# Attention and quantised FFN on one core: transposing x on TensorE, and weight quotients on GpSimd

## The reference

```
q = ctx @ Wq.T + bq ;  k = ctx @ Wk.T + bk          (512 x 128)
p = softmax(q @ k.T)                                (512 x 512)
x = x + layernorm(x) @ p.T
v = bf16(layernorm(x)) ;  h = bf16(layernorm_w_b(v))
h = bf16(quant(h) @ quant(W1).T + b1)               (512 x 2048)
h = gelu(h)
h = bf16(quant(h) @ quant(W2).T + b2)
x = x + bf16(v + h)
```

## Time and profile before

| | us |
|---|---|
| median of three runs | 285.61 (285.0 to 285.69) |
| the profiled execution | 283.25 |
| its span in the trace | 281.4 |
| busy: DVE | 249.2 (89% of the span) |
| busy: PE | 228.7 (81%) |
| busy: ACT | 169.4 (60%) |
| busy: POOL | 69.0 (25%) |

### The profile page before, as it was taken

The page is one execution under the profiler, slowest core; times in us unless marked ns, Lnnn a source line. Parts: engine busy times, 40 slices in busy tenths (PEclk is TensorE's granted clock), DMA queues, the critical chain, the costliest instruction groups (busy, mean ns, idle before and its releaser), DMA issues.

```text
span 281.4 us, 3244 instructions
## 1 busy us (share of the span) xinstructions
PE 228.7 (81%) x937; PEld 99.4 (35%) x946; DVE 249.2 (89%) x377; ACT 169.4 (60%) x287; POOL 69.0 (25%) x96
## 2 busy tenths in 40 slices
...
DMA packets 103077, 42.92 MB, mean 152 GB/s; under 512 B 93844, under 2 KB 96152, under 8 KB 102552
## 3 DMA queue, kind: packets, MB, share of 16 engines
...
## 4 chain that ended last, share of the span: by engine, by line
DVE 45%; PE 25%; ACT 11%; DMA 8%; issue 5%; POOL 4%; SPq 2%; ACTq 0%; DVEq 0%; POOLq 0%
DVE amax L764 12%; PE ps L722 9%; PE ps L712 8%; PE ps L661 4%; DVE w_int L807 4%; DMA xhl<-pf 3%; DVE hq L966 3%; DVE stats L918 3%; DMA wst<-in_L_ffn_W 3%; DVE vw L961 3%; DVE pf L871 3%; DVE phl L942 2%; DVE wquant L861 2%; POOL rs L350 2%; DVE xhl L954 2%
## 5 line engine op out<-in xcount | busy, mean ns | idle before, releaser
L661 PE MATMUL ps<-pT,xT 128*128 128x512 f16 x192 | 49.7, 414 | 14.1 <-DMA pT<-phl 11.0
L722 PE MATMUL ps<-w2T,xhl 128*128 128x512 bf16 x247 | 56.5, 379 | 2.9 <-DMA xhl<-pf 2.4
L712 PE MATMUL ps<-w1T,cxT 128*128 128x512 bf16 x256 | 58.0, 380 | 0.0
L558 ACT ACTIVATE wst<-ps 128x1024 bf16<-128x1024 f32 x32 | 32.3, 1019 | 27.9 <-PE ps L712 27.9
L764 DVE TENSOR_REDUCE amax<-phl 128x64 f32<-128x2048 bf16 x16 | 36.5, 2280 | 6.9 <-ACT phl L562 6.9
L649 PE MATMUL ps<-qkT 128*128 128x512 f32 x32 | 19.5, 715 | 22.7 <-ACT pf L457 18.8
L661 PEld LDWEIGHTS ps<-pT,xT 128*128 128x128 f16 x192 | 19.9, 106 | 48.0 <-issue 31.8
L722 PEld LDWEIGHTS ps<-w2T,xhl 128*128 128x128 bf16 x256 | 24.6, 98 | 33.2 <-DMA xhl<-pf 4.2
L712 PEld LDWEIGHTS ps<-w1T,cxT 128*128 128x128 bf16 x256 | 23.7, 98 | 32.6 <-issue 6.2
L562 ACT ACTIVATE phl<-wst 128x2048 bf16<-128x2048 bf16 x16 | 30.6, 1910 | 1.3
L423 POOL TENSOR_TENSOR wst<-wst,vs 128x512 bf16<-128x512 bf16 x12 | 14.8, 1233 | 55.5 <-DVE wquant L866 55.5
...
## 6 DMA issues: line engine op xcount, KB each, us to landing
wst<-in_L_ffn_W ACTq DMA_DIRECT2D x6, 1024.0 KB, 6.1
xs<-in_x SPq DMA_DIRECT2D x4, 1024.0 KB, 8.4
...
wst<-in_L_ffn_W SPq DMA_DIRECT2D x2, 1024.0 KB, 10.3
xhl<-pf SPq DMA_TRANSPOSE x17, 4.3
xT<-xhl SPq DMA_TRANSPOSE x16, 4.6
pT<-phl SPq DMA_TRANSPOSE x16, 3.3
```

Of the source, the lines that this page charges most:

```text
L558: act.activation(ys[:, k, 1024 * g:1024 * g + 1024], ps_y[:, 2 * g:2 * g + 2, :], ACT.Copy)\
L661: pe.matmul(ps_pv[:, t % 2, :], xT[:, t, NT * a + n, :], pT[:, :, NT * c + n, :], start=(s == 0), stop=False)
L712: last = pe.matmul(ps_y[:, c, :], h1T[:, k, t, :], w1T[:, 4 * c:4 * c + 4, t, :], start=False, stop=(t == KT - 1))
L722: last = pe.matmul(ps_z[:, k, :], h2T[:, k, t, :], w2T[:, t, :], start=False, stop=(t == FT - 1))
```

## The change

Three things are changed.

1. The transpose of normalised x. PE transposes the float32 tile `xn` in four blocks of 128 x 128 into PSUM (`transpose_x`), into `ps_xT`, which is banks 2 and 3, those of q and k. ACT then copies the high half from PSUM, and DVE subtracts from PSUM for the low half. The sixteen DMA transposes of x go. Batches alternate between two buffers, `xhl` and `xT`. `queries_keys(b)` now waits until all four `x_low` of the batch before have read the banks.
2. The weight quotients. POOL multiplies the quarter by the inverse scale in place and in float32 (`over_scale`, eight calls). DVE's clip reads that float32 and writes int16. `w_over` goes.
3. The orders. POOL's small factors stand in a new sequence with the quotients, and some of them behind a wait for a whole tail (`h_rdy`). ACT's `v` work is one step later in its loop. DVE takes the moments of the next batch in the middle of `front` and aggregates them near its end, and the tails follow the whole fronts. SP loads x of batches 2 and 3 behind the first transpose of p, not the last.

The core of the diff (PE, ACT, POOL, SP and the weight steps of DVE):

```diff
-W_STEPS = 7
+W_STEPS = 6
...
+xT_even = xhl[:, :, :, :].rearrange("p t a n -> p t (a n)").rearrange("p t (c l) -> p t c l", l=P)
+xTs = (xT_even, xT)
...
+ps_xT = ps[:, 2:4]
...
-        for t in range(LT):
-            wait_alone(sp, x_lo, b * LT + (t + 1), sp_gate)
-            wait_alone(sp, pv_ps, (b - 1) * LT + (t + 1), sp_gate)
-            sp.dma_start_transpose(xT[:, t, :, :], xhl[:, t, :, :].rearrange("p a n -> p (a n)"))\
-              .then_inc(xT_rdy[t], 16)
-            if ctx is not None and t == 0:
-                load_ctx(ctx)
+        if ctx is not None:
+            load_ctx(ctx)
         wait_alone(sp, pv_ps, b * LT, sp_gate)
         for t in range(NT):
             wait_alone(sp, p_lo, b * NT + (t + 1), sp_gate)
             sp.dma_start_transpose(pT[:, t, :, :], phl[:, t, :, :].rearrange("p a n -> p (a n)"))\
               .then_inc(pT_rdy[t], 16)
-        if later is not None:
-            load_x(later)
+            if later is not None and t == 0:
+                load_x(later)
...
+    def over_scale(a, u):
+
+        pool.wait_ge(w_step[a], W_STEPS * u + 4)
+        w = blocks(wst[:, a, :])
+        inverse = mxi[:, a, :, 0:1].broadcast_to([P, NB, BLOCK])
+        pool.tensor_tensor(w, w, inverse, ALU.mult).then_inc(w_u[a], 1)
+
+    over_scale(W1, 0)
...
+    pool.wait_ge(p_lo, NT)
+    over_scale(W2, 0)
+    over_scale(W1, 1)
+    factors_x(2)
+    mean_x1(0)
+    pool.wait_ge(p_lo, 2 * NT)
+    over_scale(W2, 1)
+    factors_x1(0)
+    over_scale(W1, 2)
+    factors_x(3)
+    factors_v(0)
+    mean_x1(1)
+    pool.wait_ge(h_rdy, LT)
+    over_scale(W2, 2)
+    factors_x1(1)
+    over_scale(W1, 3)
+    factors_v(1)
+    mean_x1(2)
+    pool.wait_ge(h_rdy, 2 * LT)
+    over_scale(W2, 3)
+    factors_x1(2)
+    factors_v(2)
+    mean_x1(3)
+    factors_x1(3)
+    factors_v(3)
...
+        act.wait_ge(xT_ps, b * LT + (t + 1))
+        wait(act, pv_ps, (b - 2) * LT + (t + 1))
+        act.activation(xTs[b % 2][:, t, 0:NT, :].rearrange("p n l -> p (n l)"), ps_xT[:, t % 2, :], ACT.Copy)\
+           .then_inc(x_hi, 1)
...
-        for t in range(LT + 1):
+        for t in range(LT + 2):
             if t < NT:
                 exp(front, t)
                 x_high(front, t)
-            if t > 0:
+            if 0 < t <= NT:
                 p_high(front, t - 1)
-            if b is not None and t > 1:
+            if b is not None and 1 < t < LT + 1:
                 x_plus(b, t - 2)
-            if t == 2 and b is not None:
+            if t == 1 and b is not None:
                 load_w2(front)
-            if v is not None and t > 0:
-                v_sums(v, t - 1)
-            if v is not None and t < LT:
-                v_out(v, t)
+            if t == LT and front + 1 < B:
+                load_w1(front + 1)
+            if v is not None and t > 1:
+                v_sums(v, t - 2)
+            if v is not None and 0 < t <= LT:
+                v_out(v, t - 1)
             if qk is not None and t == 2:
                 context(qk)
-        if not isinstance(front, int) or front + 1 < B:
-            load_w1(front + 1)
...
     def queries_keys(b):
+        wait(pe, x_lo, b * LT)
...
+    def transpose_x(b, t):
+        pe.wait_ge(xn_rdy, b * LT + (t + 1))
+        wait(pe, x_lo, b * LT + (t - 1))
+        for n in range(NT):
+            last = pe.transpose(ps_xT[:, t % 2, P * n:P * n + P], xn[:, t % 2, P * n:P * n + P], ident[:, :])
+        last.then_inc(xT_ps, 1)
...
-        pe.wait_ge(xT_rdy[t], 16 * (b + 1))
+        pe.wait_ge(x_lo, b * LT + (t + 1))
         wait(pe, x1_rdy, b * LT + (t - 1))
...
-        for t in range(LT):
-            if t < NT - 2:
-                energies(front, t + 2)
-            if b is not None:
-                values(b, t)
+        energies(front, 2)
+        transpose_x(front, 0)
+        transpose_x(front, 1)
+        if b is not None:
+            values(b, 0)
+        energies(front, 3)
+        transpose_x(front, 2)
+        if b is not None:
+            values(b, 1)
+        transpose_x(front, 3)
+        if b is not None:
+            values(b, 2)
+            values(b, 3)
...
-    def w_over(a, u):
-        dve.wait_ge(w_step[a], W_STEPS * u + 4)
-        inverse = mxi[:, a, :, 0:1].broadcast_to([P, NB, BLOCK])
-        dve.tensor_tensor(blocks(w_int[:, :]), blocks(wst[:, a, :]), inverse, ALU.mult)\
-           .then_inc(w_step[a], 1)
-
     def w_clip(a, u):
-        dve.wait_ge(w_step[a], W_STEPS * u + 5)
-        dve.tensor_scalar(w_int[:, :], w_int[:, :], QMAX, None, ALU.min).then_inc(w_step[a], 1)
+        wait(dve, w_step[1 - a], W_STEPS * (u + a))
+        dve.wait_ge(w_u[a], u + 1)
+        dve.tensor_scalar(w_int[:, :], wst[:, a, :], QMAX, None, ALU.min).then_inc(w_step[a], 1)
 
     def w_mult(a, u):
         wait(dve, (w1T_rdy, w2T_rdy)[a], 16 * u)
-        dve.wait_ge(w_step[a], W_STEPS * u + 6)
+        dve.wait_ge(w_step[a], W_STEPS * u + 5)
...
+    def x_moments(b):
+        dve.wait_ge(ld_x[b], 16)
         for t in range(LT):
             dve.bn_stats(stats[:, t, :], xs[:, LT * b + t, :]).then_inc(st, 1)
-        if isinstance(b, int) and b > 0:
+
+    def x_aggregate(b):
+        if b > 0:
             dve.wait_ge(rx_rdy, b)
+            dve.wait_ge(xn_rdy, LT * b)
         for t in range(LT):
             wait_alone(dve, st, LT * b + (t + 1), dve_gate)
             dve.bn_aggr(mv[:, t, :], stats[:, t, :]).then_inc(mvr, 1)
...
-        wait_alone(dve, x_lo, b * LT + (t - 1), dve_gate)
+        wait(dve, xT_ps, b * LT + (t - 1))
...
     def x_low(b, t):
         dve.wait_ge(x_hi, b * LT + (t + 1))
-        dve.tensor_tensor(xhl[:, t, 1, :], xn[:, t % 2, :], xhl[:, t, 0, :], ALU.subtract)\
-           .then_inc(x_lo, 1)
+        xt = xTs[b % 2][:, t, :, :]
+        dve.tensor_tensor(xt[:, NT:2 * NT, :].rearrange("p n l -> p (n l)"), ps_xT[:, t % 2, :],
+                          xt[:, 0:NT, :].rearrange("p n l -> p (n l)"), ALU.subtract).then_inc(x_lo, 1)
```

More of the change, by code:

```diff
@@ L168, in xattn_ffn_kernel @@
         nm, off_rdy = sem("nm"), sem("off_rdy")
+        w_u = [sem("w1_u"), sem("w2_u")]
         v_mean, v_mean2, v_ms = sem("v_mean"), sem("v_mean2"), sem("v_ms")
         rx_rdy = sem("rx_rdy")
-        xT_rdy = [sem(f"xT_rdy{t}") for t in range(LT)]
+        xT_ps = sem("xT_ps")
         pT_rdy = [sem(f"pT_rdy{t}") for t in range(NT)]
@@ L266, in _ @@
             front(1, 3, 3)
-            with sp.Fori(2, B) as b:
+            for b in range(2, B):
                 front(b)
@@ L399, in _ @@
             factors_x(1)
-            def batch(b, x, v):
-                if x is not None:
-                    factors_x(x)
-                if v is not None:
-                    factors_v(v)
-                mean_x1(b)
-                factors_x1(b)
-            batch(0, 2, None)
-            for b in range(1, B - 2):
-                batch(b, b + 2, b - 1)
-            batch(B - 2, None, B - 3)
-            factors_v(B - 2)
-            mean_x1(B - 1)
-            factors_x1(B - 1)
-            factors_v(B - 1)
+            pool.wait_ge(p_lo, NT)
[23 more added lines that the diff above has]
+            factors_v(3)
             def add_residual(i):
@@ L1015, in front @@
                 x_low(b, 2)
[L1016 to L1020 removed]
+                w_mult(W1, b)
                 recip(b, 3)
+                w_amax(W2, b)
+                recip_scaled(b, 3)
                 p_low(b, 2)
[L1024 removed]
+                w_power(W2, b)
                 x_low(b, 3)
[L1026 to L1049 removed]
+                w_scale(W2, b)
[4 more added lines that the diff above has]
+            def tail(b):
+                for t in range(LT):
+                    times_w(b, t)
+                    plus_b(b, t)
             def tail_parts(b):
```

86 lines of the change are left out of this document (12 added, 74 removed).

## The result

The changed kernel takes 300.91 us (median of four runs, 297.03 to 305.98) against 285.31 on the same chip: ratio 1.0537, 95% interval 1.0465 to 1.0608. The profiled execution took 300.17, its span is 298.4 against 281.4. Two of the changed kernel's four runs were in a slower state and are left out of the ratio. Executions of one kernel differ by several microseconds: those four lie within 9 us, and those of the kernel before lie within 1.5 us on this chip and within 6 on the chips of the experiments. A few tenths of a per cent between two kernels mean nothing, and the experiments are read by stretch, each from one profiled execution. T0 to T3 are the first `negmax` of the four batches, "last tile" is `x_plus(3,3)`.

The account below looks back on a forecast made before the run. Stage one was taken as a DVE queue with PE close behind, stage two as following PE. Terms 8.5 + 2.9 + 1.5 + 7.1 = 20.0 us on 283.25 gave 303.3, with 2.4 to the median 305.6; range 292 to 312.

Parts of the forecast that it names:

- Front 0: First batch's front: late first factors, late fourth exponential and q and k waiting for x_low move T1 by 8.5 us.
- The link: Between batches: q and k share PSUM banks with transposed x, so wait for the fourth x_low; 8.1 us to first energy.
- T1 to T2: Front 1: PE's in-order transposes, values, q and k, with a POOL hold on DVE, move T2 by another 2.9 us.
- T2 to T3: Front 2 and tail: ACT's later v_sums delay factors_v and the tail, moving T3 by 1.5 us.
- T3 to the last tile: Front 3 onward: POOL's last quotient and factors_x1(2) queue behind h_rdy, delaying ACT; +7.1 us.
- The sign "`x_plus(3,0)` over 20 us late": Entry of the last stretch on ACT: a delay over 20 us was to show the forecast right.
- Costed at nothing: PE's 64 blocks (8 us, up to 15), x loads (at most 8.4 us) and SP's sixteen shed transposes add nothing separately.
- DVE's saving is idle: DVE in stage one: the 3.5 us saved on it become idle time; net saving of work 14.0 us.
- The milder one: Rival: same chains without POOL holds on DVE (-5.4) and with PE at high clock at T1 (-2.7); 297.5 us, chance 0.25.
- The slow clip: Rival: DVE's clip reads float32 one element a step, 6.6 us more over three fronts; 312 us, chance 0.10.
- "Same": Rival: every new wait at its least, and the last stretch gives it back; 285 us, chance 0.04.
- "faster": Rival: DVE's queue still sets everything, 14.0 us less work minus 1.8 of first factors; 273.4 us, chance 0.05.

Follow-up runs that it names:

- e7_qk_banks: Changed kernel with q and k in PSUM banks 0 and 1 and no wait of queries_keys for the fourth x_low; ratio 1.052 to the kernel before.
- The relatives with the same front: Two variants of the changed kernel whose front 1 is unchanged, e1_factors_first and e6_v_step_early; T1 to T2 29.1 and 28.5 us.
- e9_before_pool_quotient: Kernel before with only the eight weight quotients moved to POOL in float32, x by DMA and orders of PE, ACT, SP untouched; ratio 1.028.
- e6_v_step_early: Changed kernel with ACT's v_sums and v_out one step earlier in its loop, as in the kernel before; ratio 1.049.
- e1_factors_first: Changed kernel with factors_x1(2) on POOL moved ahead of the wait for the tail and the last quotient; ratio 1.044 to the kernel before.
- e4_x_loads_last: Changed kernel with the x loads of batches 2 and 3 back behind the fourth p transpose; ratio 1.056 to the kernel before.
- e15_x_loads_first: Changed kernel with four edits of order, plus x loads of batches 2 and 3 right behind the context load; ratio 1.000 to the kernel before.
- e13_x_by_dma: Changed kernel with x transposed by DMA again, POOL's quotients and all new orders kept; ratio 1.093 to the kernel before.
- four edits of order: Changed kernel with context behind x tile 1, factors_x1(2) before the tail wait, W1's maxima and load earlier, ACT's v work one step earlier; ratio 1.004.

## Why the prediction was right, and where not

The forecast was +20.0 us on the profiled execution and 305.6 in all; +16.9 and 300.91 were measured. The direction, the four waits and their causes are right. The size owes something to errors that cancel, as said in the terms:

- **Front 0, +8.5 forecast, +5.4 measured** (+6.1 counted from T0). Right in form: the exponential is 2.2 us late (2.3), q and k wait for `x_low`, and from their start to the energy's end are 7.1 us (8.1), mostly at the low clock. The link is shown by `e7_qk_banks`. Mis-sized: POOL's quotient, 4.5 taken and 3.64 measured, below both bounds, which were scaled from 512 elements. The first factors are therefore 0.8 us late in the front and not 1.8; a T0 0.7 us earlier and the shorter link are most of the rest. Left out: the load of W1, issued 4.6 us later. It costs 1.23 us in the open (in the next stretch), and 4.5 to 7.1 as soon as T1 is earlier.
- **T1 to T2, +2.9 forecast, +5.1 measured.** The relatives with the same front give +2.0 and +2.5; the rest is 1.23 us for W1 and the `values(0,0)` at the low clock. T2 is 10.6 us later where 11.4 was forecast, and that this is so near is partly luck: in the relatives it is 8.8 us later. The order on PE (transposes behind normalisations, four `values`, q and k) is as forecast. The hold of a normalisation is real but 0.5 us and not 1.4, since the quotient is 0.9 us shorter. (In front 2, where DVE waits for no load, it is 0.5 as well.) The Trainium skill, "Advanced Engine Details and Errata", section VectorE Performance Modes, says that the second port of VectorE is shared with GpSimd, and that GpSimd's instructions and VectorE's two-port ones block each other. The trace agrees for the normalisation, most plainly in `e9_before_pool_quotient` with 3.48 for 0.54 us.
- **T2 to T3, +1.5 forecast, -1.0 measured.** The wait for POOL ahead of the tail is there (5.08), and ACT's later step costs 1.2 (`e6_v_step_early`), but the chain from T2 to T3 was summed 2.5 us too long: 1.4 by DVE's front (the fourth scaled reciprocal is at T2 + 20.0, not 21.4, mostly by the shorter hold), 0.2 by ACT, 0.5 by `factors_v` and 0.3 by the tail.
- **T3 to the last tile, +7.1 forecast, +7.0 measured.** The queue behind `h_rdy` is the cause, shown by `e1_factors_first`. The fit of the number is luck, two errors of equal size. `x_plus(3,0)` is 7.7 us late in the stretch, where 10.3 were forecast. From there to the last tile are 16.4 us, where 13.9 were forecast: the product with W1 behind 6.50 us of idle PE took 6.26 us at the low clock and not 3.63, a term that the sum doesn't have. The sign "`x_plus(3,0)` over 20 us late" was missed: it is 17.3 us late in all.
- **Costed at nothing.** The x loads: right as far as the times show (`e4_x_loads_last`, `e15_x_loads_first`). The 64 blocks on PE: 11.4 us, in the chains. The transposes that SP sheds, with their gain hidden: right for the sum, but `e13_x_by_dma` shows that without them the new orders fail.
- **DVE's saving is idle:** right for what the change does. Yet its two parts are gains within the new orders (2.0% and 3.7%), and the quotients alone are a loss in the old ones (2.8%). What the prediction did not see is that parts and orders belong together, and that four edits of order win back as much as the whole loss.
- **The rivals.** The milder one left out all holds (5.4 us) and the low clock at T1. The clock was low; the normalisations were held by 0.5, 0.5 and 0.7 us. The outcome lies between it and the forecast. The slow clip fell: 1.216 us. "Same" and "faster" fell with the waits of 5 to 7 us at T1, T2 and the tails.
- **The noise.** The prediction took 0.3% as what can be told, from three runs. The runs of the kernel before spread over 2% on other chips.
